# Four half-size last jobs, one product moved to VectorE, and a new order of turns

## The chip, the core and the metric

The kernel runs on one core of one Trainium2 chip. The metric is device time in microseconds, the median of several executions. The core has five instruction queues that matter here, each in order: PE (TensorE), DVE (VectorE), ACT (ScalarE), POOL (GpSimd) and SP, which issues all DMA transfers of the program. They meet only at semaphores: an instruction whose semaphore has not come blocks everything behind it on its own queue.

## What is computed

An input of 8 batches of 256 tokens with 128 features goes through eight residual sublayers: spiking attention, a feed-forward with FP4 quantization, a state-space block of four layers, a ternary feed-forward, linear attention, a mixture of eight experts, a diagonal state-space convolution with a LayerNorm, and a feed-forward with product keys. The change touches the last sublayer, cut to its core here:

```python
q = einsum('btd,ed->bte', x, W_q).reshape(b, t, 2, 4, 64).transpose(2, 0, 1, 3, 4)
sim = einsum('pbthn,hkpn->pbthk', q, keys)            # 2 x 4 heads x 64 keys
(sx, sy), (ix, iy) = top_k(sim, 8)
scores, pk = top_k(sx[..., :, None] + sy[..., None, :] (as 64), 8)
indices = take_along_axis(ix[..., :, None] * 64 + iy[..., None, :] (as 64), pk)   # clamped at 511 by the gather
w = silu(einsum('btd,bthkd->bthk', x, down_embed[indices]) * softmax(scores))
out = silu(x @ W_up.T) @ W_down.T + einsum('bthk,bthkd->btd', w, up_embed[indices])
```

## The kernel before, in words

Every batch is a chain of stages. Two lines of work, `a` and `b` (`Os`, tiles `o0` and `o1`, PSUM banks `ps2`/`ps3` and `ps4`/`ps5`), run all stages but the state-space block, one batch at a time each. The block runs on two more lines: `front` (`f`; projections, PSUM bank `ps1`) and `scan` (`s`; bank `ps0`, the two-bank PSUM tile `dtuB`, and most of the SBUF tile `m`). A scan of one unit (one batch, one layer; 32 units in all) has eight groups. In a group ACT makes the decays (L1027), DVE a product (L1044) and the scan (L1052), POOL the product with C (L1062) into one of six buffers `G`, and PE sums (L1081). SP brings the operands: the front writes its B and C rows to DRAM (L871), two copies spread them (L878: first B, then C), and eight copies (L1003) replicate the time steps over partitions. The copy of C waits for POOL's product in the last group of the unit two before.

All matmuls of the experts' stage are at L1444, L1448 and L1456, those of the ternary feed-forward at L1183.

The last stage, `L3Ffn`, does a batch of 256 tokens: LayerNorm, queries for both blocks of 128 tokens (L1730), then block 0 and after it block 1, since both share the buffers of a line. A block: similarities (L1739), a copy (L1688), the eight largest of each of eight groups (L1589) with their places (L1593) and what belongs to them (L1596 to L1599), the 64 sums as products of exponentials (L1607 to L1617), and then for each of four heads a table of 512 entries, one per expert. For a head POOL multiplies two rows of exponentials (L1665, `Em`), DVE masks the experts' scores with it (L1630, `md`), POOL multiplies both (L1670), ACT applies SiLU (L1707), and PE transposes and sums over heads (L1768). `Em` has two buffers, so heads 2 and 3 wait for the transposes of heads 0 and 1; `md` has one. At the end ACT copies (L1718), PE multiplies with `up_embed` (L1774), DVE adds (L1639) and SP writes the batch out (L1781).

What stands in which order on a queue is written out by hand of a program in `ORDER`: for each queue a string of letters with counts, each letter one turn of that line, which issues the instructions up to the next `yield`.

## Time and profile before

| | us |
|---|---|
| median of three runs | 1812.58 |
| the three runs | 1812.49, 1812.58, 1823.68 |
| span of the profiled execution | 1807.1 |
| the median less that span | 5.5 |

The profiled execution is given by its span, from the first instruction to the last; the page states no other time of it. The program begins with about 100 us before the first scan, then the scans run until 1577 us, with the other stages of the batches beside them; what follows is the rest of the last two batches, and from 1716 us on their last stages. Shares over the whole span mix these stretches, so they are read one by one.

### The profile page before, as it was taken

What the parts mean: (1) busy time and instruction counts of PE and PEld (TensorE: products, weight loads), DVE (VectorE), ACT (ScalarE), POOL (GpSimd) and SP (SyncE); (2) the same over time, 40 slices, a digit from 0 to 9 for tenths busy, and PEclk for the clock granted to TensorE, in tenths of its full rate; (3) what the DMA queues carried; (4) which work ended last, traced back from release to release, by engine and by line L of the source; (5) the groups of instructions that cost most, each with busy time, mean ns of one, the idle gap of its engine ahead of it and who ended that gap; (6) DMA issues with size and microseconds to landing.
All of it is one profiled execution on the core that took longest, in us unless ns stands there. A gap on an engine that the chain in (4) does not pass through costs nothing.

```text
span 1807.1 us, 27511 instructions
## 1 busy us (share of the span) xinstructions
PE 1480.0 (82%) x9545; PEld 1061.4 (59%) x9545; DVE 1436.8 (80%) x2200; ACT 1338.4 (74%) x2742; POOL 1210.7 (67%) x999
## 2 busy tenths in 40 slices
PE   5677677667899996676879999689899977899975
PEld 2343333345677775444557777566677755677854
DVE  4679999999988899889998778887998998611154
ACT  4468657757998887786788878798998887744453
POOL 4148659876777688886667667887778978800055
PEclk9678768778999998687999999899999988899987
DMA  5023412523443542221444543242544513122200
GB/s 198 1 71 72 117 39 82 117 71 107 128 135 95 173 117 58 71 71 39 117 119 127 147 121 93 59 137 72 162 106 136 158 47 92 47 83 74 99 1 6
DMA packets 84585, 170.10 MB, mean 94 GB/s; under 512 B 9440, under 2 KB 14944, under 8 KB 84064
## 3 DMA queue, kind: packets, MB, share of 16 engines
q1 hardware_dynamic: 84448, 168.36, 33.4%
q8 instruction: 76, 1.25, 0.3%
q14 instruction: 61, 0.50, 0.1%
HBM read 99.11 MB, written 2.10 MB: 56 GB/s over the span
## 4 chain that ended last, share of the span: by engine, by line
PE 46%; DVE 21%; ACT 17%; POOL 8%; issue 5%; DMA 2%; SPq 0%; DVEq 0%; POOLq 0%; ACTq 0%
DVE m L1052 9%; ACT m L1027 5%; PE ps L1444 5%; PE ps L966 5%; PE ps L1456 5%; DVE dtuB L1044 4%; ACT L345 4%; PE ps L1081 3%; PE ps L1183 3%; PE ps L1315 3%; POOL o L1670 2%; POOL o L1665 2%; PE ps L713 2%; ACT o L670 2%; PE ps L700 2%
## 5 line engine op out<-in xcount | busy, mean ns | idle before, releaser
L1062 POOL TENSOR_TENSOR m<-m 128x1024 f32<-128x1024 f32 x256 | 768.9, 3008 | 84.8 <-DVE m L1052 84.4
L1052 DVE TENSOR_TENSOR_SCAN m<-m,dtuB 128x1024 f32<-128x1024 f32 x256 | 584.9, 2285 | 18.6 <-ACT m L1027 5.6
L1027 ACT ACTIVATE m<-m,Aneg 128x255 f32<-128x255 f32 x1024 | 427.6, 497 | 24.5 <-DMA m<-m 23.2
L1044 DVE TENSOR_TENSOR dtuB<-m 128x1024 f32<-128x1024 f32 x256 | 342.5, 1338 | 13.1 <-DMA m<-m 5.0
L345 ACT ACT_TABLE_LOAD x188 | 241.2, 1283 | 3.3
L362 POOL TENSOR_TENSOR o<-o,mhalf 128x2 f32<-128x2 f32 x64 | 19.7, 308 | 222.1 <-DVE o L356 222.1
L1081 PE MATMUL ps<-m,w_const 128*32 128x256 f32 x2048 | 148.7, 415 | 5.7 <-POOL m L1062 5.7
L1425 ACT ACTIVATE o<-ps,w_mo 128x256 f32<-128x256 f32 x256 | 106.2, 471 | 51.0 <-PE ps L1448 50.9
L1444 PE MATMUL ps<-o 128*128 128x256 f32 x512 | 138.2, 392 | 6.8 <-ACT o L1425 5.2
L966 PE MATMUL ps<-m,wc 128*128 128x256 f32 x512 | 136.2, 425 | 6.2 <-ACT m L383 6.2
L1456 PEld LDWEIGHTS ps<-o 128*128 128x128 f32 x1024 | 128.6, 191 | 16.3 <-issue 4.9
L1456 PE MATMUL ps<-o 128*128 128x128 f32 x1024 | 136.4, 277 | 0.4 <-DMA o<-in_mox 0.3
L1768 PE MATMUL ps<-w_const,o 128*128 128x128 f32 x512 | 90.0, 340 | 55.8 <-DVE o L1636 36.1
L1183 PE MATMUL ps<-o 128*128 128x256 f32 x512 | 121.9, 385 | 10.4 <-issue 5.1
L966 PEld LDWEIGHTS ps<-m,wc 128*128 128x128 f32 x512 | 108.3, 216 | 30.6 <-ACT m L383 10.0
L1768 PEld LDWEIGHTS ps<-w_const,o 128*128 128x128 f32 x512 | 81.7, 245 | 67.6 <-ACT o L1707 45.4
L670 ACT ACTIVATE o<-ps 128x512 f32<-128x512 f32 x112 | 66.3, 593 | 68.2 <-PE ps L713 42.4
L713 PE MATMUL ps<-o 32*128 32x256 bf16 x224 | 55.9, 344 | 74.1 <-ACT o L670 60.9
L1183 PEld LDWEIGHTS ps<-o 128*128 128x128 f32 x512 | 93.2, 190 | 31.5 <-issue 14.8
L1081 PEld LDWEIGHTS ps<-m,w_const 128*32 128x32 f32 x2048 | 70.0, 118 | 70.3 <-issue 26.1
L1444 PEld LDWEIGHTS ps<-o 128*128 128x128 f32 x512 | 88.4, 190 | 26.7 <-ACT o L1425 12.6
L1670 POOL TENSOR_TENSOR o<-o 128x512 f32<-128x512 f32 x64 | 89.2, 1394 | 21.5 <-DVE o L1630 20.4
(246 smaller groups left out, 2783.8 us busy)
## 6 DMA issues: line engine op xcount, KB each, us to landing
m<-m SPq DMA_DIRECT2D x256, 256.0 KB, 4.9
m<-spread SPq DMA_DIRECT2D x64, 512.0 KB, 5.0
o<-in_mox SPq DMA_DIRECT2D x128, 256.0 KB, 3.4
o<-in_l1x SPq DMA_DIRECT2D x88, 256.0 KB, 2.9
w_mb<-in_mb SPq DMA_DIRECT2D x1, 2288.0 KB, 12.1
m<-in_cwr SPq DMA_DIRECT2D x1, 2048.0 KB, 16.0
w_l3f<-in_l3f SPq DMA_DIRECT2D x1, 1536.0 KB, 17.4
X<-in_x SPq DMA_DIRECT2D x4, 256.0 KB, 7.2
```

The source lines that it names most:

```text
L345: e.preload_act_table_set(SETS[kind])
L966: op = e.matmul(b[:, h * CH:h * CH + CH], wc[:, l, j, h * 128:h * 128 + 128], v.xT[:, j:j + CH], start=j == 0, stop=j == 3)
L1027: op = e.activation(dA[at % NA][:, j, 1:CH], R[q][:, h * CH + 1:h * CH + CH], ACT.Exp, scale=Aneg[:, l, 4 * g + j:4 * g + j + 1])
L1044: e.tensor_tensor(dtuB[:, :, :], bc(R[q][:, (2 + h) * CH:(3 + h) * CH].unsqueeze(1), 4, CH), Br[k % 2], ALU.mult).then_inc(S.dve, n.tick(f ...
L1052: e.tensor_tensor_scan(flat(G[at % NG]), flat(dA[at % NA]), flat(dtuB[:, :, :]), 0.0, ALU.mult, ALU.add).then_inc(S.dve, n.tick(f"s{g}"))
L1062: e.tensor_tensor(G[at % NG], G[at % NG], Cr[k % 2], ALU.mult).then_inc(S.pool, n.tick(f"c{g}"))
L1081: op = e.matmul(S.y[32 * q:32 * q + 32, h * CH:h * CH + CH], red, G[(8 * k + g) % NG][:, j, :], start=False, stop=j == 3, skip_group_check ...
L1183: op = e.matmul(b[:, 0:CH], v.ring[(at + j) % RING][:, cut(k)], src[:, k, :], start=k == 0, stop=k == 3)
L1444: e.matmul(b[:, j * CH:j * CH + CH], v.ring[p // 2 * 2 % MRING][:, cut(p % 2 * 2 + j)], v.xT, start=j == 0, stop=False, skip_group_check=True)
L1456: op = e.matmul(a[:, cut(i)], v.hd[p % 2][:, j, cut(i)], v.ring[(p // 2 * 2 + 1) % MRING][:, cut(p % 2 * 2 + j)], start=False, stop=p == 1 ...
L1670: e.tensor_tensor(v.Em[h % 2], v.Em[h % 2], v.md, ALU.mult).then_inc(T.pool, n.tick(f"w{i}{h}"))
L1768: op = e.matmul(a[:, cut(k)], v.Em[h % 2][:, cut(k)], ident, start=h == 0 and k == 0, stop=h == 3, skip_group_check=True)
```

## The change

- For the last two batches the last stage is no longer one job of 256 tokens on a line, but two jobs of 128 tokens (`L3Half`). One is on the batch's own line (`a` or `b`), the other on one of two new lines, `c` and `d`. These use the memory and the PSUM of the scan and the front (`c`: `ps0`, `ps1`; `d`: `dtuB`), and wait for the last unit of the front. Each job writes its 128 tokens out by itself.
- In these four jobs DVE does the second product of a head, in place on `Em` (after: L1862), where POOL did it (L1670). POOL keeps the first (L1665, after: L1894).
- The transposes of the heads, in all batches, carry `is_transpose=True`.
- `ORDER` is new for all queues.

```diff
@@ ORDER: one string of turns for each queue; the last of DVE's old and new lines @@
...
-        "b7",
+        "b2afbababsbs2a2bs2bs2abs2a3b8s4b4a2f2b2a4b4a4b10a7cb4cbac2b2c2da2c2a2b2cb4acb3d6a3dbd2c3b2a3d2cdbad",
...
+        Ps = [line(f"o{2 + i}") for i in range(2)]
+        for i, T in enumerate(Ps):
+            T.mem = mem[:, i * MO_:(i + 1) * MO_]
+        Ps[0].banks = ps[0:2]
+        Ps[1].banks = [flat(dtuB[:, 2 * i:2 * i + 2, :]) for i in range(2)]
...
-            v.st, v.mv, v.ve, v.rs, v.nb = V.get(2, 6), V.get(2, 2), V.get(2), V.get(2), V.get(2)
+        def norm_views(v, V, blocks=2):
+            v.st, v.mv, v.ve, v.rs, v.nb = V.get(blocks, 6), V.get(blocks, 2), V.get(blocks), V.get(blocks), V.get(blocks)
+            v.blocks = blocks
...
                         for k in range(4):
-                            op = e.matmul(a[:, cut(k)], v.Em[h % 2][:, cut(k)], ident, start=h == 0 and k == 0, stop=h == 3,
+                            op = e.matmul(a[:, cut(k)], v.Em[h % 2][:, cut(k)], ident, is_transpose=True, start=h == 0 and k == 0, stop=h == 3,
                                           skip_group_check=True)
...
+        class L3Half(Stage):
+            def __init__(self, T):
+                v, V = self, Views(T.mem, MO_)
+                v.T = T
...
+            def dve(self, e, n, c, i):
+                v, T = self, self.T
...
+                else:
+                    e.wait_ge(F.dve, F.done(after[NB - 1][1]))
+                from_, job = ready[c]
+                e.wait_ge(from_.dve, from_.done(job))
+                yield from norm_dve(e, n, T, v, X[:, 2 * c + i:2 * c + i + 1, :])
...
+                for h in range(4):
+                    if h:
+                        e.wait_ge(T.dve, n.dve(f"W{h - 1}"))
+                    e.wait_ge(T.pool, n.pool(f"E{h}"))
+                    if h == 0:
+                        e.wait_ge(T.pe, n.pe("D"))
+                    e.scalar_tensor_tensor(v.md, v.Em[h % 2], v.s8[:, h, 7:8], o[:, :], ALU.is_ge, ALU.mult).then_inc(
+                        T.dve, n.tick(f"w{h}"))
+                    e.wait_ge(T.dve, n.dve(f"w{h}"))
+                    e.tensor_tensor(v.Em[h % 2], v.Em[h % 2], v.md, ALU.mult).then_inc(T.dve, n.tick(f"W{h}"))
+                    yield
+                    if h == 0:
+                        e.tensor_copy(v.d5, o[:, 511:512]).then_inc(T.dve, n.tick("d5"))
+                e.wait_ge(T.act, n.act("w2"))
+                e.tensor_tensor(v.Em[0][:, 511:512], v.Em[0][:, 511:512], v.w5, ALU.add).then_inc(T.dve, n.tick("a5"))
+                yield
+                e.wait_ge(T.pe, n.pe("ue"))
+                e.tensor_tensor(Xi, a[:, 0:128], Xi, ALU.add).then_inc(T.dve, n.tick("x"))
+                yield
...
+            def pool(self, e, n, c, i):
+                v, T = self, self.T
+                norm_pool(e, n, T, v)
+                yield
+                e.wait_ge(T.dve, n.dve("mk"))
+                e.tensor_tensor(v.e64, v.al, v.msk, ALU.mult).then_inc(T.pool, n.tick("e"))
+                yield
+                e.wait_ge(T.act, n.act("ss"))
+                for p in range(2):
+                    if p:
...
+                    for h in (2 * p, 2 * p + 1):
+                        if p:
+                            e.wait_ge(T.pe, n.pe(f"t{h - 2}"))
+                        Eh = v.Em[h % 2].rearrange("p (a b) -> p a b", a=8)
+                        e.tensor_tensor(Eh, bc(v.s3[:, h, 0:8].unsqueeze(2), 8, 64), bc(v.s3[:, 4 + h, :].unsqueeze(1), 8, 64),
+                                        ALU.mult).then_inc(T.pool, n.tick(f"E{h}"))
+                        yield
...
+                for p in range(2):
+                    for h in (2 * p, 2 * p + 1):
+                        Eh = v.Em[h % 2]
+                        table(e, "silu")
+                        e.wait_ge(T.dve, n.dve(f"W{h}"))
+                        e.activation(Eh, Eh, ACT.Silu, scale=v.rinv[:, h:h + 1]).then_inc(T.act, n.tick(f"w{h}"))
...
+                for h in range(4):
+                    e.wait_ge(T.act, n.act(f"w{h}"))
+                    if h == 0:
+                        e.wait_ge(T.dve, n.dve("d"))
+                    if h == 2:
+                        e.wait_ge(T.dve, n.dve("a5"))
+                    for k in range(4):
+                        op = e.matmul(a[:, cut(k)], v.Em[h % 2][:, cut(k)], ident, is_transpose=True, start=h == 0 and k == 0, stop=h == 3,
+                                      skip_group_check=True)
+                    op.then_inc(T.pe, n.tick(f"t{h}"))
+                    yield
...
+            def sp(self, e, n, c, i):
+                T = self.T
+                e.wait_ge(T.dve, n.dve("x"))
+                e.dma_start(xout[:, 2 * c + i:2 * c + i + 1, :], X[:, 2 * c + i:2 * c + i + 1, :]).then_inc(out_done, 16)
                 yield
...
-                todo += [(T, s, c) for s in (PRE if word[0] == "a" else POST)]
+                todo += [(T, s, c) for s in (PRE if word[0] == "a" else POST if c < NB - 2 else POST[:-1])]
...
+        for c in (NB - 2, NB - 1):
+            T = next(T for T, s, d in todo if d == c and s is L3Attn)
+            ready[c] = (T, len(T.jobs) - 1)
+            T.add(L3Half(T), c, 0)
+            P = Ps[c % 2]
+            P.add(L3Half(P), c, 1)
...
-        lines = {"u": U, "s": S, "f": F, "a": Os[0], "b": Os[1]}
+        lines = {"u": U, "s": S, "f": F, "a": Os[0], "b": Os[1], "c": Ps[0], "d": Ps[1]}
```

Line 1052 of before is L1058 after, and so on: six more. In the new jobs the masking is L1859, the product L1862, the head's first product L1894, the transposes L1975 and the last matmuls L1981.

DVE at the end of the program (`o0`, `o1`: the lines a and b; `m`: the lines c and d), before:

```order
L1617 TENSOR_REDUCE o1<-o1 128x4
L1619 RECIPROCAL o1<-o1 128x4
L1630 SCALAR_TENSOR_TENSOR o1<-o1,ps5 128x512
L1634 COPY o1<-ps5 128x1
L1630 SCALAR_TENSOR_TENSOR o1<-o1,ps5 128x512 x3
L1636 TENSOR_TENSOR o1<-o1 128x1
L1639 TENSOR_TENSOR X<-ps4,X 128x128
```

and the change, where the four jobs take turns:

```order
L1859 SCALAR_TENSOR_TENSOR o0<-o0,ps3 128x512
L1862 TENSOR_TENSOR o0<-o0 128x512
L1867 TENSOR_TENSOR o0<-o0 128x1
L1859 SCALAR_TENSOR_TENSOR m<-m,dtuB 128x512
L1862 TENSOR_TENSOR m<-m 128x512
L1859 SCALAR_TENSOR_TENSOR m<-m,dtuB 128x512
L1862 TENSOR_TENSOR m<-m 128x512
L1870 TENSOR_TENSOR X<-ps0,X 128x128
L1867 TENSOR_TENSOR m<-m 128x1
L1870 TENSOR_TENSOR X<-ps4,X 128x128
L1870 TENSOR_TENSOR X<-ps2,X 128x128
L1870 TENSOR_TENSOR X<-dtuB,X 128x128
```

The masking and the product of a head now stand next to each other on DVE, and behind the last pair of line `d` stand only additions.

PE at the end, before (L1768 x8 are two heads):

```order
L1739 MATMUL ps5<-w_l3f,o1 128x128 x4
L1743 MATMUL ps5<-w_l3f,o1 128x512
L1768 MATMUL ps2<-w_const,o0 128x128 x8
L1774 MATMUL ps2<-w_l3f,o0 128x128 x4
L1768 MATMUL ps4<-w_const,o1 128x128 x16
L1774 MATMUL ps4<-w_l3f,o1 128x128 x4
```

and the change:

```order
L1981 MATMUL ps0<-w_l3f,m 128x128 x4
L1975 MATMUL ps2<-w_const,o0 128x128 x8
L1981 MATMUL ps4<-w_l3f,o1 128x128 x4
L1981 MATMUL ps2<-w_l3f,o0 128x128 x4
L1975 MATMUL dtuB<-w_const,m 128x128 x8
L1981 MATMUL dtuB<-w_l3f,m 128x128 x4
```

Before, only the last two heads and the last matmuls of one batch were left; now two heads of `o0` and three groups of last matmuls stand ahead of the last two heads, those in `dtuB`.

SP in the second, third and fourth scan, before (`spread<-m` is L871, `m<-spread` the copies of B and C, `m<-m` the replicas):

```order
L871 DMA spread<-m 32x256
L878 DMA m<-spread 128x1x1024 x2
L1003 DMA m<-m 128x1x512 x8
L871 DMA spread<-m 32x256
L878 DMA m<-spread 128x1x1024 x2
L1003 DMA m<-m 128x1x512 x8
```

and the change:

```order
L877 DMA spread<-m 32x256
L884 DMA m<-spread 128x1x1024
L1009 DMA m<-m 128x1x512 x8
L884 DMA m<-spread 128x1x1024
L877 DMA spread<-m 32x256
L884 DMA m<-spread 128x1x1024 x2
L1009 DMA m<-m 128x1x512 x8
```

The copy of C (the second `m<-spread` of a unit) stood ahead of the replicas of its scan, and now in these units behind all eight. Over the 32 units it stood behind four or more of the eight in 5 before, and does in 15 now.

On DVE, 734 of 1190 turns of before stand at the same place of the string, and ahead of the last turn of the last scan DVE has played 228 and 220 turns of the lines a and b before, 226 and 216 now.

## Rows read from the trace of the kernel before

**Rows 1.** The page, part 1: busy time, share of the span, instructions.
```profile
PE 1480.0 (82%) x9545; PEld 1061.4 (59%) x9545; DVE 1436.8 (80%) x2200; ACT 1338.4 (74%) x2742; POOL 1210.7 (67%) x999
```

**Rows 2.** Stretches: length, busy time (instructions) of each engine, PEclk, DMA share, GB/s.
```profile
300.00:600.00 300.00, 249.63 (x1660) 172.01 (x1651) 272.53 (x314) 237.26 (x501) 227.53 (x145) 0.90 0.41 110
...
1640.00:1660.00 20.00, 20.00 (x154) 15.44 (x154) 0.00 (x0) 8.71 (x19) 0.00 (x0) 1.00 0.13 45
...
1700.00:1720.20 20.20, 19.96 (x128) 16.90 (x126) 6.60 (x21) 11.01 (x25) 5.59 (x14) 1.00 0.20 66
1720.20:1734.10 13.90, 9.98 (x39) 6.20 (x38) 8.37 (x35) 7.40 (x14) 4.40 (x10) 0.88 0.01 2
1734.10:1807.10 73.00, 44.30 (x237) 36.72 (x236) 33.66 (x123) 33.73 (x54) 45.71 (x48) 0.80 0.01 4
```

**Rows 3.** Order of time, DVE: start, us, line, operation, [idle before, releaser].
```profile
1720.19 0.42 DVE L1403 TENSOR_TENSOR X<-ps,X 128x256 f32<-128x256 f32 x1 [2.68 <-PE ps L1456]
...
1733.64 0.43 DVE L1521 TENSOR_TENSOR X<-X,o 128x256 f32<-128x256 f32 x1
...
1742.63 1.11 DVE L1589 MAX8 o<-o 128x8 f32<-128x64 f32 x8 [0.39 <-ACT o L1688]
```

**Rows 4.** Order of time, all engines, the last 10 us.
```profile
1797.72 1.26 POOL L1670 TENSOR_TENSOR o<-o 128x512 f32<-128x512 f32 x1 [0.86 <-DVE o L1630]
...
1797.96 3.91 PE L1768 MATMUL ps<-w_const,o 128*128 128x128 f32 x16 [3.44 <-DVE o L1636]
1799.02 0.72 ACT L1707 ACTIVATE o<-o 128x512 f32<-128x512 f32 x1 [1.40 <-POOL o L1670]
...
1802.54 1.16 PE L1774 MATMUL ps<-w_l3f,o 128*128 128x128 f32 x8 [0.68 <-ACT o L1718]
1803.73 0.29 DVE L1639 TENSOR_TENSOR X<-ps,X 128x128 f32<-128x128 f32 x1 [5.93 <-PE ps L1774]
1804.05 0.91 SPq L1781 DMA_DIRECT2D out<-X  x2
```

**Rows 5.** Groups by line and form, 1734.1 to 1807.1: xcount, busy us, mean ns, idle before.
```profile
L1768 PE MATMUL ps<-w_const,o 128*128 128x128 f32 x128 | 23.9, 354 | 17.0 <-DVE o L1636 10.4 <-ACT o L1707 6.3
...
L1670 POOL TENSOR_TENSOR o<-o 128x512 f32<-128x512 f32 x16 | 20.2, 1265 | 6.0 <-DVE o L1630 6.0
...
L1630 DVE SCALAR_TENSOR_TENSOR o<-o,ps 128x512 f32<-128x512 f32 x16 | 11.9, 746 | 21.8 <-POOL o L1670 12.0 <-POOL o L1665 9.8
...
L1589 DVE MAX8 o<-o 128x8 f32<-128x64 f32 x24 | 3.3, 211 | 2.4 <-ACT o L1688 2.4
...
L1599 DVE TENSOR_TENSOR o<-o 128x512 f32<-128x512 f32 x3 | 2.0, 682 | 0.0
```

**Rows 6.** Order of time: a POOL product, and one DVE product beside and without it.
```profile
1763.43 2.66 POOL L1665 TENSOR_TENSOR o<-o 128x512 f32<-128x512 f32 x2 [2.93 <-PE ps L1768]
...
1763.92 1.27 DVE L1607 TENSOR_TENSOR o<-o 128x256 f32<-128x256 f32 x1
...
1751.54 0.43 DVE L1607 TENSOR_TENSOR o<-o 128x256 f32<-128x256 f32 x1 [0.21 <-ACT o L1698]
```

**Rows 7.** Groups by line and form, PE, 1600 to 1700.
```profile
L1347 PE MATMUL ps<-w_l2a,o 128*128 128x128 f32 x8 | 1.2, 275 | 0.0
...
L441 PE MATMUL ps<-w_const,o 128*128 128x128 f32 x8 | 1.2, 272 | 0.0
```

**Rows 8.** The page, part 5: costliest groups, the three of the scan.
```profile
L1062 POOL TENSOR_TENSOR m<-m 128x1024 f32<-128x1024 f32 x256 | 768.9, 3008 | 84.8 <-DVE m L1052 84.4
L1052 DVE TENSOR_TENSOR_SCAN m<-m,dtuB 128x1024 f32<-128x1024 f32 x256 | 584.9, 2285 | 18.6 <-ACT m L1027 5.6
...
L1044 DVE TENSOR_TENSOR dtuB<-m 128x1024 f32<-128x1024 f32 x256 | 342.5, 1338 | 13.1 <-DMA m<-m 5.0
```

**Rows 9.** The page, part 6: issues, KB each, us to landing.
```profile
m<-spread SPq DMA_DIRECT2D x64, 512.0 KB, 5.0
```

**Rows 10.** Waits, 0 to 1570: us in total, times, longest us.
```profile
ACT m L1027 <- DMA m<-m: 23.2, 8, 5.4
```

More of the change, by code:

```diff
@@ L250 @@
+        "bfs5asfas2a2s2fs6fa7fa2sbas3bs2a5fa4babs3asaf2ab3s2b7fs5b6sb3abf2sb2sbs2fs3fas5bfs3fs5afbs2afs4fs5afb2s2fs7fs3bf"
+        "s3afa3s6fa9s2asbfsfba5ba4sabsfas4b4fb3sbfbsbas4b4abfb5s2bsfs2as2fs5fs2bs4f2bs5fs4fsbs2fs6fs5afsa2sfabs4bsa4ba5baf"
+        "s2a9b2ab5ab2s2bs3b4s3b6aba2b3a4cb4dc4b4a3bcd4bca3d2",
 }
@@ L330, in cut @@
             return slice(i * 128, i * 128 + 128)
-        before, after = [None] * NB, [None] * NB
+        Ps = [line(f"o{2 + i}") for i in range(2)]
[3 more added lines that the diff above has]
+        Ps[1].banks = [flat(dtuB[:, 2 * i:2 * i + 2, :]) for i in range(2)]
+        before, after, ready = [None] * NB, [None] * NB, [None] * NB
         held = [""]
@@ L345, in table @@
                 e.preload_act_table_set(SETS[kind])
-        def norm_views(v, V):
-            v.st, v.mv, v.ve, v.rs, v.nb = V.get(2, 6), V.get(2, 2), V.get(2), V.get(2), V.get(2)
+        def norm_views(v, V, blocks=2):
+            v.st, v.mv, v.ve, v.rs, v.nb = V.get(blocks, 6), V.get(blocks, 2), V.get(blocks), V.get(blocks), V.get(blocks)
+            v.blocks = blocks
         def norm_dve(e, n, T, v, src, p=""):
-            for i in range(2):
+            for i in range(v.blocks):
                 e.bn_stats(v.st[:, i, :], src[:, i, :]).then_inc(T.dve, n.tick(f"{p}st{i}"))
-            for i in range(2):
+            for i in range(v.blocks):
                 e.wait_ge(T.dve, n.dve(f"{p}st{i}"))
@@ L359, in norm_pool @@
         def norm_pool(e, n, T, v, p=""):
-            e.wait_ge(T.dve, n.dve(f"{p}mv1"))
-            e.tensor_tensor(v.ve, v.mv[:, :, 1], mhalf[:, 2:4], ALU.add).then_inc(T.pool, n.tick(f"{p}ve"))
-            e.tensor_tensor(v.nb, v.mv[:, :, 0], mhalf[:, 4:6], ALU.mult).then_inc(T.pool, n.tick(f"{p}ng"))
+            b = v.blocks
+            e.wait_ge(T.dve, n.dve(f"{p}mv{b - 1}"))
+            e.tensor_tensor(v.ve, v.mv[:, :, 1], mhalf[:, 2:2 + b], ALU.add).then_inc(T.pool, n.tick(f"{p}ve"))
+            e.tensor_tensor(v.nb, v.mv[:, :, 0], mhalf[:, 4:4 + b], ALU.mult).then_inc(T.pool, n.tick(f"{p}ng"))
             e.wait_ge(T.pool, n.pool(f"{p}ve"))
-            e.tensor_tensor(v.rs, v.ve, mhalf[:, 0:2], ALU.pow).then_inc(T.pool, n.tick(f"{p}rs"))
+            e.tensor_tensor(v.rs, v.ve, mhalf[:, 0:b], ALU.pow).then_inc(T.pool, n.tick(f"{p}rs"))
             e.wait_ge(T.pool, n.pool(f"{p}rs"))
@@ L370, in norm_act @@
             e.wait_ge(T.pool, n.pool(f"{p}nb"))
-            for i in range(2):
+            for i in range(v.blocks):
                 e.activation(dst[:, i, :], src[:, i, :], ACT.Identity, bias=v.nb[:, i:i + 1],
@@ L1816, in _ @@
             play(e, "sp")
-            e.wait_ge(out_done, 16 * NB)
+            e.wait_ge(out_done, 16 * (NB + 2))
         @block.tensor
```

191 lines of the change are left out of this document (156 added, 35 removed).

## The prediction

> **What bounds the kernel now.** Start with the page's busy shares [rows 1]: PE 82% and DVE 80%, neither near full, which says only that the bound changes along the program. So the next view is busy time by stretch [rows 2]. Between 300 and 600 us, with scans running, DVE is busy 272.5 of 300 us: it sets the pace, PE stands at 250. Between 1640 and 1660 the scans are over, DVE does nothing and PE is busy all of the 20 us at full clock. This goes on to 1720.2, where PE ends the last batch's experts. From there nothing is full: in the last 73 us PE has 44.3, POOL 45.7, DVE and ACT 33.7 each, and PE's granted clock drops to 0.80. This is the stretch that four smaller jobs are aimed at, and the only one with much room.
>
> Third view, the order of time on DVE [rows 3]. The last batch leaves the experts at 1720.2, its convolution stage gives X at 1734.1, and 8.5 us later (1742.6) DVE can take the first maxima of its last stage. The two blocks of a batch then follow one another, and two batches share the engines.
>
> Fourth, what the heads wait for [rows 5]. DVE's masking (L1630) stood idle 21.8 us for POOL, ACT's SiLU and PE's transposes waited behind it. A head goes around five engines, with one `md` and two `Em`, and POOL's second product (1.27 us) is its longest step. It is latency on a loop with few jobs in it, and not an engine at its limit.
>
> **The end, part by part.** I work from X at 1734.1 of the profiled execution, since PE's experts ahead of it are the same work in the same order and PE has no slack there [rows 2]: up to that point the last stretch neither gains nor loses. The first jobs' matmuls stand behind the last experts' matmul, and DVE's early work for batch 6 fits in its 5.5 us of idle time between 1720.2 and 1734.1 as it did before.
>
> *DVE becomes the bound.* It had 33.7 us of work from 1734.1 on [rows 2]. The change adds 16 products. No row shows this product on DVE: 128x512, both operands in SBUF, f32. Bounds: L1599, a subtraction of the same size in SBUF, takes 0.68 us [rows 5], the low end. High end: the same plus what a collision with POOL costs. L1607 took 0.43 us with POOL idle and 1.27 beside a POOL product [rows 6], so 0.68 + 0.84 = 1.52. At 0.68 the 16 products are 10.9 us. One block's maxima now come before 1734.1 (24 such instructions take 3.3 us, so eight save 1.1) [rows 5]. DVE: 33.7 + 10.9 - 1.1 = 43.5, of which some 1.3 (four additions to X, one small one) stand behind the last product. So 42.2 us of work up to it.
>
> *Collisions.* POOL keeps 45.7 - 20.2 = 25.5 us of work [rows 2, 5], half of the about 50 us that are left. With all 16 products hit, 16 x 0.84 = 13.4 us; with half of them hit, 6.7; since in some collisions it will be POOL that waits, I take 5, and keep 0 and 13.4 as ends.
> The Trainium skill ("SBUF — State Buffer", on the port pair shared by VectorE and GpSimd) says that a VectorE instruction with two SBUF inputs and a GpSimd one that reads SBUF exclude each other for a whole instruction. This speaks against the move. The trace agrees by its 1.27 against 0.43 us. By the rule in its strict form the two engines' SBUF work would be added rather than laid side by side, which is the upper end above.
>
> *Idle.* Ahead of the maxima of the last batch's first job DVE now has about 5.6 us of work in its order (batch 6's two jobs; my estimate, a dozen instructions between the 0.2 us of one maximum and the 0.68 of L1599 [rows 5]), and these maxima cannot come before the 8.5 us of [rows 3]: 2.9 us idle. Later waits (for POOL's sums, for E of heads 2 and 3) have another job's work ahead of them, and I count nothing: what hides each is the masking and product of a neighbour, 1.43 us a head; uncovered, such a wait is about 1 us.
> Last product ends at 1734.1 + 42.2 + 2.9 + 5 = 1784.2.
>
> *After the last product.* Before: POOL's last product ends at 1799.0, the execution at 1807.1, so 8.1 us [rows 4], with transposes at the lower clock (3.9 us for two heads; the mean of 0.354 us a matmul [rows 5] lies between both levels). Now PE has two heads and two groups of last matmuls of other jobs right ahead of the last two heads. At full clock this delays them by about 1 us, at half clock by up to 6; I take 2.4. Three more output transfers cost nothing: three jobs finish earlier and the last one's transfer ends the program as before, now half as large. End: 1784.2 + 8.1 + 2.4 = 1794.7, against 1807.1: **12.4 us less**. With the ends of the unknown costs: 1734.1 + 42.2 + 2.9 + 8.1 + 1 = 1788.3 (19 less) and 1734.1 + 42.2 + 2.9 + 13.4 + 8.1 + 6 = 1806.7 (nothing).
>
> *`is_transpose`.* The call `e.transpose` sets the same flag. L441 goes through it, L1347 is an ordinary matmul of the same form, both at full clock: 272 and 275 ns [rows 7]. I take no gain from it, here and in the six batches before.
> The Trainium skill ("TensorE: Matmul & The Clock Gate", Terms) calls the transpose mode four times faster for FP32. By this the 3.9 us of the last two heads would become 1.0 and the sum would gain 2.9 more. The row speaks against it.
>
> **The new order elsewhere.** POOL, PE and ACT do the same work up to the last scan, and DVE's turns stand mostly where they stood, so I expect no shift of the bound. What "late transfers" can take away is bounded by waits for them: ACT waited 23.2 us for replicas in 8 places [rows 10], but DVE waited for ACT only 5.6 us ahead of its scan and 5.0 for replicas itself [rows 8]. I take 2 us less; below, the rest of both, 10 us less; above, a rival. SP's queue: the copy of C is moved past up to eight replicas, so they no longer stand behind its wait, and C itself is late. It takes 5.0 us to land [rows 9]. Issued once the last product of the scan before is done, it has that scan's last L1052, then L1044 and L1052: 2.3 + 1.3 + 2.3 = 5.9 us [rows 8]. It just makes it, and POOL, at 3.0 us a group against DVE's 3.6, makes up 0.6 a group.
>
> **Sum**: 12.4 + 2 = 14.4 us less in the profiled execution's time. The median is 5.5 above its span, which I keep: 1812.6 - 14.4 = **1798.2**.
>
> **Rivals.**
>
> A, the new order gains in the scans. DVE is idle 9% there [rows 2], about 135 us over the 1475 us with scans. If the order takes away a tenth, 13.5 us go besides the end: 1812.6 - 12.4 - 13.5 = 1786.7. For it: every small wait of DVE counts fully there. Against: most of these waits are for PE and ACT in chains whose length no order changes. 0.2.
>
> B, collisions at full price: all 16 products pay 0.84, so 8.4 us more than the forecast, 1806.6. For it: POOL's products and DVE's belong to interleaved jobs and so run side by side all the time. Against: L1630 between them reads PSUM, which spaces them. 0.12.
>
> C, PE falls to its lower clock and becomes the bound of the end. PE has 44.3 us at a mean clock of 0.80; at half that is 44.3 x 0.80 / 0.5 = 71 us, begun some 2 us after 1734.1, then 3.4 to the end: 1810.5, so 3.4 more than before, with the 2 of the order 1814. For it: the clock fell already. Against: four jobs leave PE shorter pauses than two. 0.06.
> The Trainium skill ("TensorE: Matmul & The Clock Gate", Part 4: PE-mode transpose) says that work in transpose mode does not count as busy for the clock gate, which would produce just this. No row shows a stretch of flagged transposes alone; the chance above is mine.
>
> D, slower: the late copies of C. Ten more units than before have C behind at least half of the replicas. If it then misses the first group of the scan, POOL starts late, and DVE has to wait once the lag exceeds the six buffers of `G`, or PE's sum of the unit comes late to the front, whose next layer needs it. This decides from a landing about 1 us slower than the median. With 3.5 us lost for each of ten units: 1798.2 + 35 = 1833. Against it stand the 5.9 us and POOL's 0.6 a group. 0.06.
>
> **Chances.** Forecast 0.56, with its own range of 1790 to 1807. 1% of 1812.6 is 18 us, about what can be told from no change: faster is below 1794.5, slower above 1830.7. A and a third of the forecast's own spread lie below: 0.20 + 0.18 = 0.38. D is slower: 0.06. The rest, 0.56, is the same. The range for 8 in 10 takes in A, B and most of C: 1782 to 1813.
>
> **What would show it.** In the changed profile: L1862 at 0.68 us where POOL is idle and up to 1.5 beside it; DVE busy about 85% or more between the last X of the convolution stage and its last product, and ACT's SiLU no longer waiting for POOL; this stretch about 50 us, not 65; the flagged transposes at 272 ns at full clock; DVE's idle time up to 1577 within a few us of before; ACT's waits for replicas below 23. I am wrong if X of the last batch comes elsewhere than near 1734 (then the order did it, A or D), if L1862 is far from 0.68 to 1.5, or if PE is busy through the whole last stretch (C).

## The result, and the profile after

The changed kernel takes 1968.9 us (median of 4 runs, 1968.6 to 1970.4) against 1814.7 for the kernel before (median of 4): a ratio of 1.085, 95% interval 1.082 to 1.087, so 154 us slower. Forecast were 1798, and a chance of 0.06 for being slower by more than 1%. Later runs stand beside medians of the kernel before between 1813.4 and 1817.4, so differences of a few us between runs of different experiments mean nothing.

First the busy shares, which answer to [rows 1]. Engines do little more than before (PE 42 us, DVE 34 us more), in a span that is 160 us longer:

```profile
PE 1522.1 (77%) x9321; PEld 1066.9 (54%) x9321; DVE 1470.8 (75%) x2218; ACT 1338.1 (68%) x2743; POOL 1180.1 (60%) x991
```

Next the stretches, as in [rows 2]. The first table cuts the kernel before where its last scan ends, the second does so for the changed one and adds the stretch behind the last X of the last batch:

```profile
0.00:1577.00 1577.00, 1285.50 (x8345) 905.43 (x8346) 1372.07 (x1960) 1231.42 (x2526) 1146.18 (x902) 0.89 0.36 100
1577.00:1807.10 230.10, 194.50 (x1202) 156.01 (x1200) 64.72 (x240) 107.02 (x216) 64.51 (x98) 0.91 0.16 51
```

```profile
0.00:1752.30 1752.30, 1338.12 (x8107) 918.19 (x8108) 1391.37 (x1951) 1223.90 (x2513) 1122.28 (x892) 0.83 0.33 90
1752.30:1967.10 214.80, 184.01 (x1216) 148.67 (x1214) 79.47 (x267) 114.25 (x230) 57.82 (x100) 0.96 0.19 57
...
1915.60:1967.10 51.50, 29.68 (x182) 24.16 (x181) 44.19 (x134) 30.46 (x52) 31.04 (x36) 0.83 0.02 6
```

The whole result is in these rows. Behind the last scan the changed kernel needs 214.8 us, not 230.1: 15 less. Up to it, it needs 1752.3, not 1577.0: 175 more. DVE, which paces this part, works 1372.1 us in it before and 1391.4 after. Its idle time there is 1577.0 - 1372.1 = 204.9 and 1752.3 - 1391.4 = 360.9 us. So 156 of the 175 us are idle time of the engine that sets the pace, and 19 are more busy time, 17 of them the longer product `dtuB` of each scan (below, 256 x (1.403 - 1.338)). PE's granted clock fell from 0.89 to 0.83.

What DVE waits for, in the same stretches (us in total, times, longest us), before and after:

```profile
DVE o L1630 <- POOL o L1670: 15.6, 14, 2.6
...
DVE m L840 <- PE ps L1081: 11.0, 11, 2.3
DVE m L860 <- ACT ps L935: 9.0, 8, 3.4
...
DVE o L1120 <- ACT o L1145: 6.6, 8, 1.5
```

```profile
DVE m L846 <- PE ps L1087: 32.6, 14, 5.6
DVE m L1058 <- ACT m L1033: 30.0, 20, 5.2
DVE m L866 <- ACT ps L941: 21.7, 17, 2.6
DVE o L1636 <- POOL o L1676: 21.1, 14, 2.7
DVE o L1126 <- ACT o L1151: 17.8, 15, 3.2
```

(Line numbers of the changed kernel are 6 higher.) No single wait makes the loss. Most of them grew: PE's sum for the front, ACT's decays, the front's chain, the products of POOL in other lines' heads. And the loss is spread over all the scans: unit 8 starts at 435.8 us before and 481.1 after, unit 16 at 794.4 and 890.6, unit 31 at 1520.9 and 1697.2, which is 5.3 to 6.4 us a unit in the three stretches.

How such a unit loses time, in order of time (start, us, engine, line, [idle before, releaser]):

```profile
357.53 6.63 PE L972 MATMUL ps<-m,wc 128*128 128x256 f32 x16 [0.66 <-ACT m L389]
...
364.19 0.84 ACT L921 ACTIVATE m<-ps,w_mb 128x256 f32<-128x256 f32 x2 [2.24 <-PE ps L972]
...
366.25 0.60 ACT L926 ACTIVATE m<-ps 128x512 f32<-128x512 f32 x1 [1.22 <-PE ps L978]
...
368.00 0.37 ACT L929 COPY m<-ps 40x256 f32<-40x256 f32 x1 [0.79 <-PE ps L984]
...
368.38 1.28 ACT L349 ACT_TABLE_LOAD   x1
...
369.68 3.29 ACT L1033 ACTIVATE m<-m,Aneg 128x255 f32<-128x255 f32 x8
371.46 2.29 DVE L1058 TENSOR_TENSOR_SCAN m<-m,dtuB 128x1024 f32<-128x1024 f32 x1 [2.12 <-ACT m L1033]
```

The decays that DVE's scan needs stand on ACT's queue behind three of the front's turns, each of which waits for PE. PE's convolution took 6.63 us there at a granted clock of 0.56, near the lower of its two levels, where the same line took 3.72 at full clock (at 330.8 us, clock 1.00). The decays come late, and DVE stands still for 2.12 us.

Now the end. Last experts' X and last X, as in [rows 3], and the last 9 us, as in [rows 4]:

```profile
1903.06 0.42 DVE L1409 TENSOR_TENSOR X<-ps,X 128x256 f32<-128x256 f32 x1 [18.34 <-PE ps L1462]
...
1915.55 0.42 DVE L1527 TENSOR_TENSOR X<-X,o 128x256 f32<-128x256 f32 x1
...
1960.78 0.69 DVE L1862 TENSOR_TENSOR m<-m 128x512 f32<-128x512 f32 x1
...
1961.88 1.06 PE L1975 MATMUL dtuB<-w_const,m 128*128 128x128 f32 x8
...
1963.62 1.16 PE L1981 MATMUL dtuB<-w_l3f,m 128*128 128x128 f32 x8 [0.67 <-ACT m L1936]
1964.82 0.29 DVE L1870 TENSOR_TENSOR X<-dtuB,X 128x128 f32<-128x128 f32 x1 [2.60 <-PE dtuB L1981]
```

The products on DVE in that stretch, as in [rows 5]:

```profile
L1862 DVE TENSOR_TENSOR o<-o 128x512 f32<-128x512 f32 x8 | 6.5, 808 | 0.3
L1862 DVE TENSOR_TENSOR m<-m 128x512 f32<-128x512 f32 x8 | 6.2, 776 | 0.3
```

Last, the scan's groups, its copies and the waits for transfers, as in [rows 8 to 10]:

```profile
L1068 POOL TENSOR_TENSOR m<-m 128x1024 f32<-128x1024 f32 x256 | 758.7, 2970 | 196.4 <-DVE m L1058 171.3
L1058 DVE TENSOR_TENSOR_SCAN m<-m,dtuB 128x1024 f32<-128x1024 f32 x256 | 584.8, 2284 | 45.1 <-ACT m L1033 30.0
...
L1050 DVE TENSOR_TENSOR dtuB<-m 128x1024 f32<-128x1024 f32 x256 | 359.1, 1403 | 15.8 <-DMA m<-spread 4.6
...
m<-spread SPq DMA_DIRECT2D x64, 512.0 KB, 6.0
```

```profile
POOL m L1068 <- DMA m<-spread: 24.8, 6, 6.6
...
ACT m L1033 <- DMA m<-m: 6.0, 3, 2.4
```

The new order does shorten one kind of wait: ACT's for replicas, from 23.2 to 6.0 us. That is 17 us of ACT's time, against 156 us more idle time of DVE.

### The profile page after: what moved, and what is told of

Read it like the earlier page. It is cut to its first block, busy times and chain, and to the rows that moved or that the text cites. A ratio compares the mean times of both kernels' runs of the same rounds, so it can differ in the third digit from the quotient of the medians.

```text
span 1967.1 us, 27073 instructions
## 1 busy us (share of the span) xinstructions
PE 1522.1 (77%) x9321; PEld 1066.9 (54%) x9321; DVE 1470.8 (75%) x2218; ACT 1338.1 (68%) x2743; POOL 1180.1 (60%) x991
## 3 DMA queue, kind: packets, MB, share of 16 engines
q8 instruction: 75, 1.23, 0.3%
## 4 chain that ended last, share of the span: by engine, by line
PE 48%; ACT 22%; DVE 14%; POOL 6%; issue 5%; DMA 3%; SPq 1%; DVEq 0%; ACTq 0%; POOLq 0%
ACT m L1033 6%; PE ps L1450 5%; PE ps L972 4%; DVE m L1058 4%; PE ps L1087 4%; ACT L349 4%; PE ps L1462 4%; PE ps L1321 4%; PE ps L1189 3%; POOL m L1068 2%; DVE dtuB L1050 2%; ACT o L676 2%; PE ps L719 2%; PE ps L706 2%; PE ps L1332 2%
## 5 line engine op out<-in xcount | busy, mean ns | idle before, releaser
L1068 POOL TENSOR_TENSOR m<-m 128x1024 f32<-128x1024 f32 x256 | 758.7, 2970 | 196.4 <-DVE m L1058 171.3
L1058 DVE TENSOR_TENSOR_SCAN m<-m,dtuB 128x1024 f32<-128x1024 f32 x256 | 584.8, 2284 | 45.1 <-ACT m L1033 30.0
L1050 DVE TENSOR_TENSOR dtuB<-m 128x1024 f32<-128x1024 f32 x256 | 359.1, 1403 | 15.8 <-DMA m<-spread 4.6
L1087 PE MATMUL ps<-m,w_const 128*32 128x256 f32 x2048 | 156.8, 429 | 16.6 <-POOL m L1068 16.6
L368 POOL TENSOR_TENSOR o<-o,mhalf 128x2 f32<-128x2 f32 (+1 forms) x64 | 21.0, 329 | 240.6 <-DVE o L361 240.5
L1450 PE MATMUL ps<-o 128*128 128x256 f32 x512 | 143.9, 405 | 16.8 <-ACT o L1431 9.5
L972 PE MATMUL ps<-m,wc 128*128 128x256 f32 x512 | 142.6, 440 | 13.8 <-ACT m L389 13.8
L1189 PE MATMUL ps<-o 128*128 128x256 f32 x512 | 131.2, 408 | 22.9 <-DMA o<-in_l1x 9.8
L1462 PEld LDWEIGHTS ps<-o 128*128 128x128 f32 x1024 | 134.7, 197 | 20.0 <-issue 3.6
L1189 PEld LDWEIGHTS ps<-o 128*128 128x128 f32 x512 | 99.5, 202 | 46.8 <-issue 17.0
L1450 PEld LDWEIGHTS ps<-o 128*128 128x128 f32 x512 | 91.4, 196 | 38.7 <-ACT o L1431 19.7
L901 POOL TENSOR_TENSOR m<-m 128x512 f32<-128x512 f32 x32 | 46.6, 1455 | 81.7 <-DVE m L866 81.7
L719 PEld LDWEIGHTS ps<-o 32*128 32x128 bf16 x224 | 13.6, 99 | 134.6 <-ACT o L676 91.5
L1321 PE MATMUL ps<-o 32*128 32x128 f32 x512 | 80.6, 301 | 0.0
```

What stands on the lines that cost most here:

```text
L719: op = e.matmul(score[h % len(score)][:, kt * CH:kt * CH + CH], v.km[j][32 * g:32 * g + 32, cut(kt)], v.qk[32 * g:32 * g + 32, 0, :], star ...
L972: op = e.matmul(b[:, h * CH:h * CH + CH], wc[:, l, j, h * 128:h * 128 + 128], v.xT[:, j:j + CH], start=j == 0, stop=j == 3)
L1050: e.tensor_tensor(dtuB[:, :, :], bc(R[q][:, (2 + h) * CH:(3 + h) * CH].unsqueeze(1), 4, CH), Br[k % 2], ALU.mult).then_inc(S.dve, n.tick(f ...
L1058: e.tensor_tensor_scan(flat(G[at % NG]), flat(dA[at % NA]), flat(dtuB[:, :, :]), 0.0, ALU.mult, ALU.add).then_inc(S.dve, n.tick(f"s{g}"))
L1068: e.tensor_tensor(G[at % NG], G[at % NG], Cr[k % 2], ALU.mult).then_inc(S.pool, n.tick(f"c{g}"))
L1087: op = e.matmul(S.y[32 * q:32 * q + 32, h * CH:h * CH + CH], red, G[(8 * k + g) % NG][:, j, :], start=False, stop=j == 3, skip_group_check ...
```

## The experiments

In all of them the jobs and stages are those of the changed kernel, unless it is said otherwise, and only the strings of turns differ. "Old order" means the turns of the kernel before on all five queues up to its last scan; behind it the turns of the changed kernel follow, except in g1 to h2, where the end is ordered anew, too.

**Undoing the order, whole and by queue.** The four orders of PE, DVE, ACT and POOL belong together (a turn of one waits for turns of the others, and an old string among new ones would wait for itself), so only SP's is exchanged alone; which of the four costs most was not tried.

```diff
 # e1, on DVE's string, a piece in the middle (one letter a turn; s scan, f front, a and b the other lines)
-saabbffbbaaabffsbbsssssssssafsssssssss
+saabbfbfababaffsbbssssssssssafssssssss
 # e2: e1 with SP's string as in the changed kernel, a piece of it (e3: the reverse, in the changed kernel)
-sssssbbbbsfbbfbbssssbssssfssffsfsssss
+sbbbsssbbbbbbfffssssssssbbffssssssssffff
 # e4: the kernel before, product on DVE in the last stage of the last two batches (waits for it not shown)
+if c >= NB - 2:
+    e.wait_ge(T.dve, n.dve(f"w{i}{h}"))
+    e.tensor_tensor(v.Em[h % 2], v.Em[h % 2], v.md, ALU.mult).then_inc(T.dve, n.tick(f"W{i}{h}"))
```

> The changed kernel with the old order of turns on all five queues up to the last turn of the last scan, and the new order behind it; jobs, stages and is_transpose as changed. Theory O (the new order of turns makes every unit of the scans about 5 us longer): 1795 to 1805, the last scan ends near 1577 us, and the stretch behind it is about 14 us shorter than before. Rival N (the loss is not in the order: is_transpose in the six first batches, two more lines of semaphores): stays at 1955 or more.

> As the kernel with the old turns up to the last scan, but SP's string is the new one throughout, so that only the DMA issues stand in the new order. Theory Q (SP's order, with the copies of C behind the replicas, costs the 5 us a unit): 1940 or more. Theory O in the form that the other four queues carry the loss: 1800 to 1812.

> The changed kernel with the old string on SP alone up to the last scan, the other four queues new. Theory Q: 1800 to 1815. Theory O: 1950 or more, within 1% of 1969.

> The kernel before, with one part of the change alone: in the last two batches DVE does the second product of a head (old order, two jobs of 256 tokens). If the latency of the head's loop bounds the end, the end becomes 5 to 8 us shorter (16 products in two lines, each 0.6 us shorter and without the way to POOL and back): 1806 to 1810. If it is the count of jobs in the loop alone, no change within 2 us of 1814. The product is 0.68 us alone and up to 1.5 beside POOL.

Measured: e1 1806.7 us, a ratio to before of 0.996 (0.993 to 0.998); in its trace the stretch behind the last scan is 216.4 us, 14.7 shorter than before. e2 1888.7, e3 1954.0, e4 1814.7 (ratio 0.999, 0.997 to 1.001). So all of the loss, 162 us, is in the order of the turns, and half-sized jobs with their products on DVE cost nothing. SP's new order alone costs 82 us, between what its two theories said; put back into an otherwise new order, SP's old string gives only 15. The other four queues in the new order cost 147 us by themselves (e3 against e1), and e3's trace shows few waits for transfers: ACT's for replicas are 6.9 us in all.

The product on DVE without the split jobs does not move the median. In e4's trace the stretch behind the last scan is 225.2 us against 231.1 before, 5.9 shorter, as its first theory had it, but its last scan ends at 1588.1 us, not at 1576.0, though nothing ahead of it was edited. So the scans of the same code differ by 12 us between two executions, and a gain of 6 us at the end can't be told from the median. The split jobs without the product were not tried.

**Is it local?**

```diff
 # f1: old order for 16 units, then the new one; DVE's string where they part
-fsbsssbssbbbbbbbfbssasbaaffbbsafaabbs
+fsbssssbbbbbbfbbbsssasbaafbbfsfabbaas
```

> The changed kernel with the old order of turns on all five queues for the first 16 of the 32 units, and the new order behind. The kernel with the old order up to its last scan took 1806.7 us, the changed one 1968.9: 162 us lie in the order of the scans. Theory R (each unit is longer by itself, some 5 us, because the turns of that unit stand where no measured duration put them): half of it, 1806.7 + 16 x 5.1 = 1888 us (1875 to 1900), and the first 16 units start as in the kernel before (unit 16 near 850 us). Rival G (something gathers over the run: one early shift that all later units carry, or a clock that stays low): either nearly nothing (under 1830) or nearly all (over 1940).

Measured: 1876.9 us, 70 above e1 where 81 were expected. Unit 16 starts at 797.6 us, 3 later than in the kernel before (the 850 of the expectation was a slip). From there to unit 31, which starts at 1607.0, are 809 us, as in the changed kernel (807) and not as before (727). So every stretch pays for its own turns, and one early shift that all later units carry is excluded. That says nothing against a clock that falls where the new order runs; of that more below.

**Is it this order, or any other?** Turns were shifted at random, with no aim. The replay that the expectation names is a calculation, not a run: five queues in order, each instruction with its line's mean time in the trace of before.

```diff
 # f2, DVE's string, the same piece of the old order
-bfababaffsbbssssssssssafssssssssssfssff
+bfababffasbbsssssssssasfsssssssssfssff
 # h3: half the spread
-sabaaffbaffssfbssssssssssssssfaabfbbfs
+sabaafbfaffssfbssssssssssssssfaabfbbfs
```

> The changed kernel with the old order of turns, in which neighbours are exchanged at random: each turn's time in a replay of the old order got a random shift with a standard deviation of 0.5 us and the five queues were sorted anew. 6% of PE's turns, 8% of DVE's, 12% of ACT's and 1% of POOL's then stand elsewhere; in the new order it is 37, 24, 41 and 15%. Theory R (the old order is a fit to the durations of this machine, and exchanges of turns cost whatever they are meant for): the replay, with mean durations of the trace before, gives +66 us for it, +55 for the new order, of which the chip made 162; so 1850 to 1950 us, say 1880. Rival P (it is the direction of the new order that costs: work put ahead of what waits for the copies, since they are counted as late): exchanges without direction cost next to nothing, 1807 to 1820 us.

> As the jitter before, with a standard deviation of 0.25 in place of 0.5 us: 1% of PE's turns, 2% of DVE's and ACT's and 17% of SP's stand elsewhere than in the old order. The replay with the exclusion gives +12 us (+70 for 0.5 us, measured +125). Theory E: 1.8 x 12 = 21 us, 1820 to 1840. Rival V, a knife's edge (any change of the old order loses most of it): 1870 and more.

Measured: f2 1932.1 us, 125 above e1; h3 1840.8, 34 above, where 21 were expected, at the edge of its range; neither the rival P of the first nor the knife's edge of the second holds. The waits are of the same kinds as the changed kernel's, here f2's (lines 8 above those of before):

```profile
DVE m L868 <- ACT ps L943: 24.3, 14, 3.9
DVE m L1060 <- ACT m L1035: 20.3, 16, 5.1
DVE o L1128 <- ACT o L1153: 19.6, 13, 4.7
DVE m L848 <- PE ps L1089: 18.4, 11, 3.8
...
ACT m L1035 <- DMA m<-m: 29.0, 11, 8.9
```

Moving 8% of DVE's turns and 7 to 12% of PE's and ACT's by a place or two, for no purpose, costs most of what the new order costs, in waits of the same kinds. A spread of 0.5 us costs 125 us and one of 0.25 us costs 34, so the old order fits this chip's durations to a fraction of a microsecond, and an order that does not fit them can lose 100 us and more, whatever it is meant for.

One thing is mixed in. SP's queue was shifted, too: 19% of its turns stand elsewhere in f2 and 17% in h3, which the expectation of f2 does not name, and SP's order can cost much by itself (e2). In f2 the waits for transfers hardly grew: ACT's for replicas are 29.0 us against 23.8 in e1, and POOL never waits for C, where in e2 it does for 35.4 us. So it is likely that most of the 125 us are the other queues', but no run here jitters them with SP's string kept, and of h3's 34 us the share of SP is open.

**SP's queue.** Of its 82 us, how much are the copies of B and C?

```diff
 # f3: SP's queue, one unit of the scans
-spread<-m; m<-spread (B), m<-spread (C); m<-m x8 (replicas)
+spread<-m; m<-spread (B); m<-m x8; m<-spread (C)
```

> The changed kernel with the old order of turns; on SP's queue alone the scans' replicas and the fronts' copies of B and C stand to each other as in the new order, and the loads of the other lines keep their places. With all of SP's queue in the new order it was 1888.7 us, 82 more than with the old. Theory C (the copies of B and C, late behind replicas, or replicas behind them, are those 82 us): 1870 to 1890 us. Rival L (it is the loads of weights among the replicas, or SP held in front of a load): 1807 to 1820 us.

Measured: 1848.1 us (four runs, 1843 to 1864), 41 above e1, half of the 82; neither theory alone. The rows show a second effect beside the late C: the replicas wait, too. First e1, then f3 (lines 9 above those of before):

```profile
ACT m L1036 <- DMA m<-m: 23.8, 9, 5.2
DVE dtuB L1053 <- DMA m<-m: 4.6, 6, 1.9
```

```profile
ACT m L1036 <- DMA m<-m: 31.9, 16, 5.5
POOL m L1071 <- DMA m<-spread: 25.8, 6, 6.4
DVE dtuB L1053 <- DMA m<-m: 16.9, 9, 5.4
DVE dtuB L1053 <- DMA m<-spread: 8.4, 1, 8.4
```

The copy of C now goes out behind four or more of the eight replicas in 15 units, not in 5. The landings of both kinds hardly lengthen in the median (5.0 to 5.2 us, 4.9 to 5.5), while single waits grow up to 8.4 us. For the other half of the 82 the traces point at the loads of weights: PE waits 49 us for them in e2, in 11 places, against 5 in e1 and 20 in f3. No run moved these loads alone. The largest such wait in e2, and POOL's for C there:

```profile
PE ps L1176 <- DMA o<-in_l1x: 17.1, 3, 10.3
...
POOL m L1071 <- DMA m<-spread: 35.4, 7, 9.4
```

**The flag on the transposes.**

```diff
-op = e.matmul(a[:, cut(k)], v.Em[h % 2][:, cut(k)], ident, is_transpose=True, start=h == 0 and k == 0, stop=h == 3,
+op = e.matmul(a[:, cut(k)], v.Em[h % 2][:, cut(k)], ident, start=h == 0 and k == 0, stop=h == 3,
```

> The changed kernel with the old order of turns, and the heads' transposes as plain matmuls by the unit matrix, as in the kernel before, without the flag for a transpose. With the flag it was 1806.7 us. The trace has 272 ns (with it) and 275 ns (without) for one 128x128 product in other places. Theory T0 (the flag changes nothing): 1806.7 within 3 us. Rival T1 (a flagged transpose of f32 is cheaper by about half: 256 x 2 x 0.07 us of PE, of which the last half-jobs' part is on the path): 1809 to 1815 us.

Measured: 1808.7 us, ratio to before 0.995 (0.993 to 0.997); e1 had 0.996 (0.993 to 0.998). In the whole time the flag changes nothing that these runs can tell. In the work of PE it does. The last two heads, eight transposes, in f4 (without) and in e1 (with the flag), both at a granted clock of 1.00:

```profile
1799.04 1.95 PE L1978 MATMUL dtuB<-w_const,m 128*128 128x128 f32 x16
```

```profile
1796.37 1.07 PE L1978 MATMUL dtuB<-w_const,m 128*128 128x128 f32 x8
```

Without the flag a 128x128 product of f32 stands in the trace as two instructions, with it as one, and the eight take 1.07 us, not 1.95. Over the program PE has 256 instructions fewer and 1453.3 us of work, not 1481.9. So T0 has the time right and T1 the price of a transpose. In the end of the program some of it is on the path: from the last product on DVE to the end it is 5.6 us in e1 and 7.6 in f4.

**Can an order be made from the rows?** If the misfit is the cause, an order fitted to measured durations should undo it. The replay of above, with transfers landing as measured, was shortened by exchanging turns; what it gives is an estimate.

```diff
 # g1, DVE's string, from the new order on (g2 and g4 likewise; g3 from the old one)
-sssaabbffbbaaabffsbbsssssssssafssssssss
+sassbbsfbababfaffssbsbsssssassfssssssss
 # h1: the same start; DVE's instructions that read only SBUF and POOL's exclude each other in the replay
-saabbffbbaaabffsbbsssssssssafsssssssss
+saafbfabffbbbbbasassssssssssafssssssss
```

> The changed kernel with an order of turns found by exchanging turns, from the new order on, for the shortest replay with measured durations (means by line of the trace before, replicas landing after 4.9 us and copies of B and C after 5.0, transfers one behind the other on their engines). The replay, whose times only differ rightly and too small (it gives +94 us for the new order against the old, where the chip made +162), puts it 148 us below the new order and 54 below the old. Theory R (the new order lost because its turns do not stand where this machine's durations put them, and nothing else of the change costs): 1750 to 1830 us, in any case over 120 less than the 1968.9. Rival S (something else slows the changed kernel, or any order not tried on the chip is as bad as the new or the jittered one, 1930 and more): over 1900.

> As the run before, found in the same way, from the same order and with the same measured durations of instructions, but with the replicas and the copies of B and C counted as landing 5 us later than measured. The replay with the measured landings puts it 17 us above the order fitted to them. Theory R (it was the durations as a whole that did not fit; counting transfers late by itself buys cover cheaply): within 40 us of the run before, 1770 to 1870. Rival P (counting transfers as late is what makes an order slow on this chip, since other work goes ahead of the scan's own): 1900 us and more, most of the way back to 1968.9.

> As g1, begun at the old order and searched five times as long; the replay puts it 24 us below g1 and 78 below the old order. Theory R with a replay that is right in what it leaves out: 1730 to 1800 us, faster than the kernel before. Rival V (a replay with mean durations cannot see what the old order was fitted to on the chip; the longer the search, the more it fits the replay's own errors): 1815 us and more, slower than the old order, and not below g1.

> As g3, begun at the new order; the replay puts it 3 us above g3. It shows how far two orders of the same worth in the replay differ on the chip. Theory R: within 25 us of g3. Rival V: they differ by 40 us or more, as the jitter did.

Measured: 1930.2, 1956.3, 1927.2 and 1948.2 us. g1, g2 and g3 lie 86 to 127 us above the times that theory R gave, and all four are about as slow as the jitter; for g1 and g3 the rivals hold. g2 and g4 are mixed: g2, which counts transfers 5 us late, is only 26 us above g1, and g4 only 21 above g3, as theory R had these differences. A part of why they fail is in g3's trace. First a group of a scan as it stands in the kernel before, then g3 (DVE and POOL in order of time):

```profile
337.12 1.23 DVE L1044 TENSOR_TENSOR dtuB<-m 128x1024 f32<-128x1024 f32 x1
338.39 2.29 DVE L1052 TENSOR_TENSOR_SCAN m<-m,dtuB 128x1024 f32<-128x1024 f32 x1
```

```profile
337.17 3.38 POOL L1062 TENSOR_TENSOR m<-m 128x1024 f32<-128x1024 f32 x1 [0.21 <-DVE m L1052]
```

```profile
381.70 0.50 DVE L759 TENSOR_TENSOR o<-ps,o 128x352 f32<-128x352 f32 x1
381.86 2.35 POOL L1071 TENSOR_TENSOR m<-m 128x1024 f32<-128x1024 f32 x1 [0.21 <-DVE m L1061]
382.11 3.19 DVE L1053 TENSOR_TENSOR dtuB<-m 128x1024 f32<-128x1024 f32 x1
...
385.81 2.27 DVE L1061 TENSOR_TENSOR_SCAN m<-m,dtuB 128x1024 f32<-128x1024 f32 x1
```

Before, `dtuB`'s product follows straight on the scan, begins 0.05 us ahead of POOL's product, and takes its 1.23 us; POOL pays, 3.38 instead of 2.35 us, and has the time. In g3 one short turn stands between. POOL comes first by 0.25 us, and DVE's product takes 3.19 us: it ends 1.1 us after POOL's. The mean of this line over 256 is 1.34 us before, 1.40 in the changed kernel, 1.43 in f2, 1.51 in g1 and 1.59 in g3; the difference is 63 us of DVE's time in g3, which is 120 us above e1, and 17 us in the changed kernel. A replay with the mean duration cannot see it. With the exclusion put in:

> The changed kernel with an order refitted as in g1, from the new order on, but by a replay in which a DVE instruction with all its operands in SBUF and a POOL instruction exclude each other for their whole length, the earlier one first, each with the duration that it has alone (L1044 1.23 us, L1062 2.35). That replay puts the orders that ran on the chip in nearly their measured sequence, at 0.6 of the measured differences: +58 to 84 us for g1 to g4 (measured +120 to +150), +98 for the new order (+162), +70 for the jitter (+125), +31 for the copies of f3 (+41). It puts this order 70 us below the old one. Theory E (the exclusion is what the refits lacked): 1690 to 1790 us, faster than the kernel before. Rival V (the chip has still more that only running an order on it shows; an order that was not picked by chip times stays slow): 1840 us and more, but still below g1's 1930, since DVE's wait for POOL is gone.

> As the run before, begun at the old order; the same value in the replay within 6 us. Theory E: 1690 to 1790 us, and within 25 us of the run before. Rival V: 1840 and more.

Measured: h1 1881.6 us and h2 1872.4. The line is nearly back at its old length, here in h1 (h2: 1348 ns):

```profile
L1053 DVE TENSOR_TENSOR dtuB<-m 128x1024 f32<-128x1024 f32 x256 | 351.6, 1374 | 8.3 <-DMA m<-m 1.2
```

and the time is 46 to 84 us below the four without it, and 87 and 97 below the changed kernel. That is what rival V said: over 1840 and below g1. The exclusion was a part of what the refits lacked (against g3, 61 us less of this product and 55 us less in h2's time), and 75 and 66 us against the old order remain, for which no run names the cause. None of these orders beats the kernel before. The fastest version is e1 (f4 is its equal): the changed end behind the old order, 0.4% faster than before.

## Why the prediction was wrong, point by point

**The step that failed** is "The new order elsewhere": "DVE's turns stand mostly where they stood, so I expect no shift of the bound", worth 2 us less. It measured 162 us more (1968.9 against e1's 1806.7). The premise was nearly true, and the conclusion doesn't follow: a quarter of DVE's turns stand elsewhere, with 37% of PE's and 41% of ACT's, and f2 shows that small shifts of 8% of DVE's and of turns on the other queues cost 125 us. I bounded the loss by the waits for transfers that could be removed, at most 10 us, and never asked what the exchange of turns would uncover. The row to read for that was the busy share of [rows 2]: DVE at 272 of 300 us with PE, ACT and POOL between 227 and 250 beside it. With four engines so full, in order, and each other's suppliers, little is left to absorb a turn that stands wrongly; that is an argument from the rows, and f2 agrees with it.

**The rivals.** D, slower through the late copies of C, had the right sign and, as a mechanism of its own, about the right price: 35 us, where f3 measured 41, the longer waits for replicas among them. It is a small part of what happened: POOL's waits for C are 24.8 us in 6 places in the changed kernel, none before, and the otherwise new order hides them in greater losses (SP's old string gives back 15 of 162 us there). A, a gain in the scans, counted DVE's idle time there as something to win; it grew from 205 to 361 us. C did not happen at the end: PE's clock was 0.83, but it was busy only 29.7 of the last 51.5 us. PE's clock did fall in the scans, 0.89 to 0.83, and PE's busy time there grew by 1338.1 - 1285.5 = 52.6 us, though the flag takes work off it; against e1, which has the flag, too, it grew by 70. In f2 PE has as many instructions as in e1 (8155 up to the last scan) and 54 us more of busy time. Whether this is only a consequence of PE's longer waits or lengthens them in return was not separated: the replay, which has no clock, gives 0.6 of the measured losses, so it may be the missing part. This stays open.

**The end came out near the forecast, in part by luck.** Predicted were 12.4 us less; measured from the end of the last scan on DVE it is 15.3 less in the changed kernel (215.8 against 231.1) and 14.7 in e1 (216.4). But the terms moved more than the sum. From the end of the last X on it is 51.1 us, not 73.0: 21.9 less, where 12.4 were predicted. And from the last scan to that X, which I took as unchanged, it is 164.7 us against 158.1, 6.6 more. DVE does 36.4 us of work in it and not 31.1, a part of the half jobs' already; whether that delays X was not tried. By terms: last X to last product 50.1 us predicted, 1961.5 - 1916.0 = 45.5 measured; DVE busy 42.8 of these 45.5 us, 94% (85% or more was the sign); 16 products 12.7 us, of which collisions 1.8 by the 0.68 us of the row used, where I took 5. After the last product 10.5 us predicted, 5.6 measured: the other jobs' matmuls were done by then, and the last eight transposes took 1.06 us, where my sum kept the 3.9 of before. Rival B, collisions at full price, is refuted by L1862's 0.79 us.

**The flag.** Taken as nothing, and that was a misreading of [rows 7]. The 272 and 275 ns are of one instruction each. L441's x8 are eight transposes in 1.2 us, L1347's x8 are four products, two instructions each, in the same 1.2 us; so the row said half, not equal. f4 against e1 shows it for the same eight transposes, 1.95 and 1.07 us. The "four times faster" of the Trainium skill ("TensorE: Matmul & The Clock Gate", Terms) has the right direction; these runs show a factor of 1.8. The 1.0 us that the prediction worked out from it for the last two heads was measured, 1.06, but from 3.91 us at a granted clock of 0.52: the clock gave the first half (1.95 in f4 at full clock), the flag the second.

**The pair of ports.** I used the exclusion of DVE and POOL only for the products of the end. The Trainium skill ("SBUF — State Buffer", on the port pair shared by VectorE and GpSimd) states it for a whole instruction, and the traces agree nearly in that strict form: 1.23 or 3.19 us for one and the same product, which ended 1.09 us after POOL's. Its place was the scans, where the product runs 256 times: 37 of them take 1.3 us or more before, 47 in the changed kernel and 79 in g3.

## What to carry to other kernels

When several in-order engines are each 75 to 91% busy and feed each other, the order of their turns is part of the tuning like any size: a change that makes the order anew must be costed as a new order, with a loss of up to a tenth as a possible outcome, and an edit of the computation should keep the old order wherever it can (here: 0.4% faster in place of 8.5% slower). A random shift of a few turns is a cheap measure of how tight an order is, if each queue is shifted by itself. An order planned from mean durations misses who comes first where two engines exclude each other; here it was cheaper when POOL, which has time to spare, came second. And a count in a profile row may be of instructions, not of matmuls: divide the busy time by what the code asks for before two forms are compared.

## What the runs showed of the hardware

- A DVE product with both inputs in SBUF and a POOL product excluded each other for nearly the whole instruction, and the earlier one won: L1044 took 1.23 us when first, and 3.19 (the same line in g3) behind a POOL product of 2.35 us that began 0.25 us earlier; L1062 took 3.38 us when it began 0.05 us after L1044. The scan L1052, whose second operand `dtuB` is in PSUM, kept its 2.29 us beside POOL's product (mean of 256 in every run 2.28 to 2.29).
- Eight f32 transposes of 128x128 took 1.95 us as plain matmuls (16 instructions) and 1.07 with `is_transpose=True` (8 instructions), both at full clock.
- PE's convolution took 3.72 us for its 16 instructions at full clock and 6.63 at a granted clock of 0.56. With more waiting in the scans the mean granted clock went from 0.89 to 0.83.
- With the 512 KB copies of C sent out behind the 256 KB replicas in ten more of 32 units, the median landing of the 512 KB copies went only from 4.9 to 5.5 us, and the kernel lost 41 us.
